# Four product buffers and four PSUM banks in the edge loops of a graph network, sums accumulated three pairs behind

## What is computed

```
h_s, h_v = s @ lin1_ws * a / 8,  v @ lin1_wv * a / sqrt(32)   # per node: the table
w   = silu(edge_scalars @ fc_w1 / 8) @ fc_w2 / 8              # per edge, 224 weights
w1, w2, w3, w4, w5 = split(w, [64, 128, 160, 192])
es, ev = h_s[src], h_v[src]                                   # gathered
e0, e1 = edge_attr[:, :1], edge_attr[:, 1:4]
mid_s = [w1 * es * e0, w4 * dot(ev, e1) / sqrt(3)]                   # 96
mid_v = [(w2 * es) x e1, w3 * ev * e0, w5 * cross(ev, e1) / sqrt(2)] # 128 x 3
agg   = segment_sum([mid_s, mid_v], dst) / 4                  # 480 sums per node
```

## Time and profile before

| | us |
|---|---|
| median of three runs | 12102.8 |
| profiled execution | 12098.74 |
| its span, first to last instruction | 12096.9 |
| TensorE busy (matmuls) | 9397.7 (78%) |
| VectorE busy | 9136.3 (76%) |
| ScalarE busy | 7003.3 (58%) |
| GpSimd busy | 6367.4 (53%) |

### The profile page before, as it was taken

One profiled execution on the slowest core, in us unless ns is written; L12 is line 12 of the kernel. 1 busy time (PEld: TensorE's weight loads), 2 busy tenths in 40 slices (PEclk: granted clock), 3 DMA queues, 4 the chain that ended last, 5 costly groups with the idle time before them and its releaser, 6 DMA issues. The chain is left out here.

```text
span 12096.9 us, 245491 instructions
## 1 busy us (share of the span) xinstructions
PE 9397.7 (78%) x46500; PEld 6592.8 (55%) x46501; DVE 9136.3 (76%) x32454; ACT 7003.3 (58%) x26255; POOL 6367.4 (53%) x9502
## 2 busy tenths in 40 slices
PE   4421188888888888888888788887788888788887
PEld 1211177777777777777777344445433335444445
DVE  6702078888888888888887899995565555899996
ACT  0000067777777777777776555553566666676764
POOL 0677646666666666666542455551355553455551
PEclk9855589999999999999998999996799999999997
DMA  6433211111111111111111343333222223343333
GB/s 262 53 66 70 64 31 31 30 30 30 30 31 30 31 30 30 31 30 31 27 17 38 82 87 86 87 85 46 43 53 52 52 52 54 84 87 85 86 85 60
DMA packets 1798441, 691.91 MB, mean 57 GB/s; under 512 B 1586190, under 2 KB 1677258, under 8 KB 1798346
## 3 DMA queue, kind: packets, MB, share of 16 engines
q0 software_dynamic: 219136, 411.56, 14.6%
q1 hardware_dynamic: 1572154, 275.26, 13.5%
q10 hardware_dynamic: 7056, 4.02, 0.1%
HBM read 514.24 MB, written 171.77 MB: 57 GB/s over the span
## 5 line engine op out<-in xcount | busy, mean ns | idle before, releaser
L963 POOL DMA_INDIRECT shared<-table,rec x2640 | 2560.4, 970 | 2508.8 <-issue 1058.4
L1045 PE MATMUL bank<-tp,oh 128*128 128x480 f32 (+1 forms) x5280 | 2407.3, 552 | 6.3 <-DVE tp L1122 4.6
L997 ACT ACTIVATE tp<-tp,rec 128x64 f32<-128x64 f32 x7920 | 2030.3, 335 | 234.1 <-DVE tp L1093 153.2
L1037 PE MATMUL bank<-w_fc,hT 128*128 128x448 f32 x2640 | 1368.5, 601 | 701.5 <-ACT hT L981 447.9
L1680 ACT ACTIVATE shared<-bank 128x512 f32<-128x512 f32 x1760 | 973.6, 595 | 961.9 <-PE bank L1755 955.1
L1045 PEld LDWEIGHTS bank<-tp,oh 128*128 128x128 f32 x5280 | 921.0, 195 | 856.8 <-issue 843.5
L1755 PE MATMUL bank<-ident,tp 128*128 128x128 f32 x7040 | 1054.0, 299 | 265.5 <-ACT tp L813 218.2
L1093 DVE TENSOR_TENSOR tp<-bank,shared 128x256 f32<-128x256 f32 x1320 | 560.2, 424 | 924.3 <-PE bank L1045 613.4
L782 POOL DMA_INDIRECT rec_dst<-ACC x784 | 813.5, 1038 | 602.5 <-issue 571.9
L1755 PEld LDWEIGHTS bank<-ident,tp 128*128 128x128 f32 x7040 | 889.9, 154 | 303.3 <-ACT tp L813 253.6
L1644 POOL DMA_INDIRECT gat<-table,rec x880 | 866.7, 985 | 277.0 <-issue 190.7
(11 more groups left out here) (248 smaller groups left out, 22541.0 us busy)
## 6 DMA issues: line engine op xcount, KB each, us to landing
shared<-table,rec POOLq DMA_INDIRECT x2640
rec_dst<-tp SPq DMA_DIRECT2D x44, 900.0 KB, 23.6
ACC<-in_attrs SPq DMA_DIRECT2D x56, 623.0 KB
rec_src<-tp SPq DMA_DIRECT2D x44, 730.0 KB, 19.9
efr<-rec_src SPq DMA_DIRECT2D x440, 64.0 KB
efr<-rec_dst SPq DMA_DIRECT2D x440, 64.0 KB
ACC<-in_attrs SPq DMA_DIRECT2D x196, 130.0 KB
rec<-rec_dst SPq DMA_DIRECT2D x1320, 10.0 KB
```

The costliest lines, as they stand in the source:

```text
L963: nc.gpsimd.indirect_dma_start(out=gatx[:, u, g, 0:L.row], out_offset=None, in_=tables[L.n][:, :], in_offset=IOff(ap=rec[:, u, g, L.idx:L. ...
L997: done = nc.scalar.activation(t[:, g, lo:lo + 64], t[:, g, 0:64], ACT.Copy, scale=rec[:, u, g, L.y + k:L.y + k + 1])
L1037: nc.tensor.matmul(pW[u % 2][:, 0:448], hT[:, u % 2, :], fc2[:, :], start=True, stop=True)\
L1045: done = nc.tensor.matmul(pS[u % 2][:, 0:TW], oh[:, u, g, :], tp[:, u % 2, g, 64:64 + TW], start=g == 0, stop=g == G - 1)
```

## The change

Products get four buffers: the two in `tp`, one in `gat` and one in the free columns of `shared`. Sums get four PSUM banks, 4 to 7. Product and sums matmul of pair n wait for the sums, or the accumulation, of pair n-4 and not n-2. `keep` handles the pair three behind in place of two; after the last product three are left. Layer 2's column of ones is set in all four buffers. The weights' two banks, the orders of ScalarE, TensorE, SyncE and GpSimd and all other waits stay.

```diff
-            zeroed = mark("sums_zeroed", 2 + (L.n == 2))
+            zeroed = mark("sums_zeroed", 2 + 4 * (L.n == 2))
+            products = [tp[:, 0], tp[:, 1], gat.rearrange("p u g f -> p (u g f)")[:, 0:G * TPW].rearrange(
+                "p (g f) -> p g f", g=G), shared[:, 3136:3136 + G * TPW].rearrange("p (g f) -> p g f", g=G)]
-            pW, pS = [BK[2], BK[3]], [BK[4], BK[5]]
+            pW, pS = [BK[2], BK[3]], BK[4:8]
...
-                        nc.gpsimd.memset(tp[:, :, :, 64 + 384:64 + 385], 1.0).then_inc(zeroed.h, 1)
+                        for t in products:
+                            nc.gpsimd.memset(t[:, :, 64 + 384:64 + 385], 1.0).then_inc(zeroed.h, 1)
...
-                        t = tp[:, u % 2]
+                        t = products[u]
...
-                            pe.wait_ge(kept.h, kept.free(i, u))
-                        done = nc.tensor.matmul(pS[u % 2][:, 0:TW], oh[:, u, g, :], tp[:, u % 2, g, 64:64 + TW],
+                            pe.wait_ge(kept.h, kept.free(i, u, 4))
+                        done = nc.tensor.matmul(pS[u][:, 0:TW], oh[:, u, g, :], products[u][:, g, 64:64 + TW],
...
-                        t, w, row = tp[:, u % 2], w_of(u), gatx[:, u]
+                        t, w, row = products[u], w_of(u), gatx[:, u]
...
-                        ve.wait_ge(summed.h, summed.free(i, u))
+                        ve.wait_ge(summed.h, summed.free(i, u, 4))
...
-                        nc.vector.tensor_tensor(row, row, pS[u % 2][:, 0:TW], ALU.add).then_inc(kept.h, 1)
+                        nc.vector.tensor_tensor(row, row, pS[u][:, 0:TW], ALU.add).then_inc(kept.h, 1)
...
-                    for u in range(2):
+                    for u in range(3):
                         product(0, u, None).then_inc(tp_ready.h, 1)
-                    for u in range(2, 4):
-                        product(0, u, (0, u - 2, block_of(0, u - 2))).then_inc(tp_ready.h, 1)
+                    product(0, 3, (0, 0, block_of(0, 0))).then_inc(tp_ready.h, 1)
                     with ve.Fori(1, QP) as i:
                         for u in range(4):
-                            back = (i - 1, u + 2) if u < 2 else (i, u - 2)
+                            back = (i - 1, u + 1) if u < 3 else (i, 0)
                             product(i, u, (*back, block_of(*back))).then_inc(tp_ready.h, 1)
-                    for u in range(2, 4):
+                    for u in range(1, 4):
                         keep(QP - 1, u, block_of(QP - 1, u))
```

More of the change, by code:

```diff
@@ L1132, in keep @@
                         ve.wait_ge(kept.h, kept.free(i, u, 1))
-                        nc.vector.tensor_tensor(row, row, pS[u % 2][:, 0:TW], ALU.add).then_inc(kept.h, 1)
-                    ve.wait_ge(zeroed.h, zeroed.at(2 + (L.n == 2)))
-                    for u in range(2):
+                        nc.vector.tensor_tensor(row, row, pS[u][:, 0:TW], ALU.add).then_inc(kept.h, 1)
+                    ve.wait_ge(zeroed.h, zeroed.at(2 + 4 * (L.n == 2)))
+                    for u in range(3):
                         product(0, u, None).then_inc(tp_ready.h, 1)
-                    for u in range(2, 4):
-                        product(0, u, (0, u - 2, block_of(0, u - 2))).then_inc(tp_ready.h, 1)
+                    product(0, 3, (0, 0, block_of(0, 0))).then_inc(tp_ready.h, 1)
                     with ve.Fori(1, QP) as i:
                         for u in range(4):
-                            back = (i - 1, u + 2) if u < 2 else (i, u - 2)
+                            back = (i - 1, u + 1) if u < 3 else (i, 0)
                             product(i, u, (*back, block_of(*back))).then_inc(tp_ready.h, 1)
-                    for u in range(2, 4):
+                    for u in range(1, 4):
                         keep(QP - 1, u, block_of(QP - 1, u))
```

## The result

The changed kernel takes 12134.27 us (median of 20 runs, 12096.78 to 12187.93), the kernel before beside it 12082.39. The ratio is 1.0046 with a 95% interval from 1.0033 to 1.0058: about 52 us slower, where 12 faster was forecast. The profiled execution took 12130.36, its span 12128.5, the clock 0.897 as before.

What follows compares the result with a forecast made beforehand. It took a TensorE and ScalarE ring of 3.40 us a pair (3.28 in layer 2) as the bound of the edge loops. Gains of 8 + 4 = 12 us from 12102.8 gave 12091, range 12010 to 12150.

Steps and rivals of the forecast that it cites:

- The ring of 3.40 and 3.28: Edge loops: TensorE and ScalarE steps between weights matmuls set 3.40 us a pair in layers 1 and 3, 3.28 in layer 2.
- Rival A: Edge loops: the removed wait was in the ring after all; layers 1 and 3 fall to 3.35 a pair, 12036 us; 12%.
- The size of the lead: VectorE's product can start earlier by at most 1.25 us in layer 3, 0.83 in layer 2, 2.1 in layer 1.
- its new releasers: VectorE's product would be released by the weights matmul (L1037) or the scaling (L987), no longer by the sums (L1045).
- VectorE's durations, the new places, the add three behind at 0: Edge loops: buffers' new places and accumulation three pairs behind cost 0; VectorE's instructions keep their lengths.
- Rival C: Edge loops: VectorE's instructions become longer, through new buffer places or other instructions beside them; 12170 us; 8%.
- 12 us of gain: Three edge loops: 8 us in the middles plus 4 in the last pairs, from covering products that start late.
- the last 25 pairs: End of each edge loop: stays at 3.7 to 4.0 us a pair; the lead gains 3 x 1.2 = 4 us.
- the middles: Edge loops before their last 20 to 25 pairs: 5 us for late products plus 3 in layer 1, 8 in all.
- Pauses about as many: TensorE's idle events in the edge loops lie in its own chain and stay about as many; no term in the sum.
- rival D: Edge loops: TensorE falls to its lower clock more often, layers 1 and 3 becoming like layer 2; +200, 12300 us; 3%.
- Rival B: Edge loops: the lead takes the first 0.8 us of each of about 125 pauses, 100 us, giving 11990; 8%.

Runs made afterwards that it cites:

- the lead off: Changed kernel with the product of pair n waiting for the sums of n-2 again; ratio to the kernel before 1.0002 (base 12083), 0.9998 and 1.0003 (bases 11696, 11693).
- the quiet pair of traces: Traces of the changed kernel (0.9995) and of it with the lead off (0.9998 or 1.0003), when the kernel before took about 11695 us.
- the first pair of traces: Traces of the kernel before and of the changed kernel from the main measurement; 12082.39 against 12134.27 us, ratio 1.0046.
- the second pair: Traces of the changed kernel run again (1.0043) and of it with the lead off (1.0002), where the kernel before takes 12083 us.
- the held scalings: Changed kernel plus one ScalarE copy of 128x64 ahead of the six axes instructions per pair in layers 1 and 3; ratio 1.0082 (base 12183), 0.9996 (base 11695).

## Why the prediction was wrong

- *The ring of 3.40 and 3.28, and a removed wait outside it*: right in every trace. Rival A is out. One reading was looser than it sounds: the earlier trace rows name "issue", and not the activation, as what ends the 0.44 before the weights matmul; the changed trace does name the activation (L984).
- *The size of the lead, and its new releasers*: right. The product starts 1.11 earlier in the pair of layer 3 (1.25 was the bound).
- *VectorE's durations, the new places, the add three behind at 0*: right. L1103 and L1118 have medians of 450 and 346 ns, as L1100 and L1115 had. Rival C is out, and the runs with the lead off show it in both conditions.
- *12 us of gain*: right in sign where it can be seen by itself, and too small to be measured there. In the quiet pair of traces the three loops sum to 4468 us with the lead off and 4461 changed, 7 of the 12, but that is one execution of each, and the runs (0.9995 and 0.9996, both intervals reaching over 1) cannot tell it from nothing. Counted from weights matmul to weights matmul, about 5 of them lie in the last 25 pairs (4 was the term) and 2 to 3 in the middles (8 was the term). The last pairs run at 3.6 a pair, a little under the 3.7 I named.
- *Pauses about as many, because they lie in TensorE's own chain*: this is the step that failed; the sum had 0 for it. The first half was right: they are TensorE's. The second did not follow. That a delay arises on one engine does not say that another engine's timing leaves it alone. In the first pair of traces the stretches are 171 before and 177 changed, so in number "about as many", but they hold 273 and 312 us, 40 more; in the second pair both grow, from 140 with 237 us to 175 with 310. The spans of the first pair differ by 31.6. Of that the loops make 19, and 8 came ahead of layer 1 in code that is the same; one profile of each has a scatter of tens of us. What carries the weight is the measured +0.46% and +0.43% with the lead against +0.02% without.
- *What a pause costs*: rival D took the low clock for the cause of pauses, and the sum had no price for it as their consequence. It comes behind them and adds 1.7 us to each pair that it covers.
- *Rival B, the lead absorbs the pauses*: wrong in sign. *Rival D, TensorE falls to its lower clock more often*: it did, 224 us against 205 and 252 against 162 in the loops, but behind the late stretches and not as their source, and with 3% and 200 us against the 50 that came. My sign for it, a clock under 0.97 in layer 1 or 3, was too coarse to show it (0.99 and 0.98). The Trainium skill ("TensorE: Matmul & The Clock Gate", A second HAM failure mode: psum-queue depth-cycling) ties swings of the clock to cycling through PSUM banks. The number of banks is not what acts here: four banks with the lead off lose nothing, 1.0002.

Shown is that the lead, and not the rest of the change, makes the loss; that it goes with a TensorE that finishes late more often and longer; that this needs a condition that comes and goes. What that condition is, and by what way VectorE's timing reaches TensorE, stays open. That more work of the other engines beside TensorE brings such stretches fits the held scalings and the lead, but is argued: the lead adds no work, it only moves it, and no run separates the two. A variant that beats the kernel before in both conditions was not found: quiet, none is told from it on the fast side, and disturbed, each one with a lead loses. The kernel before is the safe one.

## What to carry to other kernels

Extra buffers that only let a non-bounding engine run ahead have little to win (here 7 us of 11690 in one pair of traces) and shift what runs beside the engine that bounds; ask of every pause on that engine whether it is a fixed event or one that depends on its neighbours, and give the second a price of its own, with what its clock loses behind each pause. Compare variants only with runs of the old kernel beside them, and look for the machine's condition first: four experiments here said "no difference" truthfully and told nothing of the loss. Put the undo of each part in one set of runs with the change itself, so that they meet the same condition.

## What the runs showed of the hardware

The same program takes 11695 us or 12083 to 12187, on the same chip at different hours, with no "remote" wait before the activation in the first and 31 to 88 in the others, and a granted clock in the middles of the loops of 1.00 against 0.94 to 0.99. That is 3.3 to 4.2%, more than the change moves. In the disturbed condition TensorE finishes a matmul 1 to 3 us late at a granted clock of 1.00, while the profile's own durations of it, which are modelled, stay 0.38 or 0.49; the idle time of the engine that waits for it shows it. The granted clock falls behind such stretches (1.00, then 0.59 in the 3.45 us behind the one of the earlier trace rows) and not ahead of them. And a ScalarE copy of 128x64 (0.34 us, the next instruction starts 0.24 later), free beside the lead in the one condition (0.9996), goes with +0.82% in the other, where the whole change without it had +0.43 to +0.46% (at a base of 12083, the copy at 12183).
